# Solving a chunk's triangular system in two halves, and products that nobody reads between the stages of a delta-rule kernel

## The chip, the cores and the metric

One NeuronCore of a Trainium2 chip runs the whole program. The metric is device time in microseconds (us); the figure of a version is the median of its runs. All arithmetic is float32.

## The reference, cut to what matters

Two transformer-like layers run over one sequence of 2048 tokens of width 128. Layer 0 mixes tokens with a spiking gated delta rule of 8 heads, 64 wide; layer 1 has windowed attention; each has a feed-forward part.

```
def step(carry, ins):                       # scanned over 2048 tokens
    mem = DECAY * mem + dt;  spike = (mem > THR);  mem = mem - spike * THR
    alpha = sigmoid(at + asp * spike)
    beta  = sigmoid(bt + sum(spike * bsp))
    active = sum(abs(spike)) > 0            # the "count of spikes" per head
    alpha = where(active, alpha, 1);  beta = beta * active
    s = s * alpha
    pred = k . s
    s = s + (beta * k) (x) (v - pred)
    out = q . s
```

The kernel computes the scan of `s` in 16 chunks of 128 tokens. Within a chunk the corrections of all tokens solve a unit lower triangular system per head, T u = v - k.S, where S is the state at the chunk's start; then out = q.S + A u, and S is decayed and updated with the chunk's keys and u.

## The kernel before, in words

The program has a setup phase, a spike phase (the membrane recurrence on VectorE), the delta phase (16 chunks) and a post phase, in which groups of 512 tokens pass the output projection and feed-forward of layer 0 ("mix") beside the windowed attention and feed-forward of layer 1 of the group before ("win"). Each engine has its own list of work, written out by hand; engines meet at counting semaphores whose steps have names (`tensor_back`, `vector_front` and so on). In the delta phase each name is one step of a chunk.

One chunk on TensorE: `base` (scores within blocks of 8 tokens, L869), `blocks` (scores between blocks at the levels 8, 16, 32, 64, L892, each with half a for the even and b for the odd heads; between 16 and 32 stands the spread product, L884, which copies the near terms to all rows), `front_beta` (L851) and `front_count` (L856, the count of spikes) for the next chunk, `transposed` (L903), then `join` at 8, 16 and 32 (L920, then L929 and L931 per half) and `last_join` at 64 (L939, L945), which double the size of the inverted blocks until the whole inverse of T stands in `tt`. `state1` (L953: what the state gives for the keys; L956: end keys to rows), `solve` (L964), `seen_by_q` (L972), `state2` (L979: output; L983: update of the state) end the chunk.

VectorE does between them: `base` (L1132 masked copies, L1123 near sums, L1138 spread input), `upper` per level and half (L1160 and L1161 at 8 and 16; L1157 at 32; L1154 at 64), the substitution within blocks of 8 in seven steps `row` and `row_sum` (L1170, L1175), with an `upper` after each of the first six, `tt` (L1193), `front_z`, `front_sums` (L1057 and, as step b1, L1046), `front_late` (L1116, L1117), the joins' differences (L1203) and sums (L1209), and, in between, the next chunk's gates and keys (`front_decay` L1063 and L1066 up to `front_upper` L1107 and L1109), then `rest` (L1216), `keep` (L1222) and `update` (L1227). ScalarE copies PSUM to SBUF (L761 spread, L751 to L757 far blocks, L766 transposes, L779 joins, L788, L792, L796, output L803) and does the exponentials (L718 to L743).

In the post phase `contract` (L1741) is a product of four accumulated parts; it waits once for all of its inputs. In the last group there is only "win" work: `scores` (L1880), `weights_to_columns` (L1890), `values` (L1914), `own` (L1899), then means and variances (L1815, L1822), `last_hidden` (L1925) and `last_out` (L1741).

## Time and profile before

| | us |
|---|---|
| median of 3 runs | 1461.54 (1457.33 to 1476.28) |
| profiled execution, its own time | 1458.59 |
| profiled execution, its span | 1456.9 |

| engine | busy us | share of the span |
|---|---|---|
| TensorE products | 1115.5 | 77% |
| VectorE | 1032.8 | 71% |
| ScalarE | 625.4 | 43% |
| GpSimd | 57.4 | 4% |

The delta phase lies between about 298 and 1049 us of the span, the post phase behind it. No engine is full, and work is handed between engines many times in a chunk: the share of an engine is read per stage. A float32 product stands in the trace as two records.

### The profile page before, as it was taken

The page shows a single profiled execution, that of the slowest core. Times are in us where ns is not written, and L with a number is a line of the kernel's source. Part 1 is how long each engine was busy: PE and PEld are TensorE (multiplying, and loading weights), DVE is VectorE, ACT ScalarE, POOL GpSimd, SP SyncE. Part 2 cuts the span into 40 slices and gives each one's busy share as a digit, 9 for nine tenths or more (in the row PEclk, how much of TensorE's full clock was granted, in tenths as well). Part 3 has the DMA queues.
Part 4 walks back from the last instruction along what each step waited for, and adds up shares of the span by engine and source line. Part 5 has one row for each costly group of instructions (what it writes and reads, how often), then busy time and mean ns, then how long its engine had stood idle before and what let it go on. Part 6 is the DMA issues. An engine that isn't in the chain of part 4 may idle for free. (4 is left out here: it accounts for less than half of the span.)

```text
span 1456.9 us, 23383 instructions
## 1 busy us (share of the span) xinstructions
PE 1115.5 (77%) x7956; PEld 821.2 (56%) x7956; DVE 1032.8 (71%) x3377; ACT 625.4 (43%) x860; POOL 57.4 (4%) x74
## 2 busy tenths in 40 slices
PE   2087777228888988889888898887876888889885
PEld 1043232117777877778777787777732635446381
DVE  4779999978788787887878878788241736454451
ACT  2247677323333433334333343333333656474522
POOL 2000000010000000000000000000100102011100
PEclk9579887558999999999999999999878998998956
DMA  2002233310100100101010010110110000000000
GB/s 84 0 1 87 105 127 145 116 51 16 36 25 33 36 14 36 35 22 36 14 36 36 22 36 14 36 36 7 30 39 0 1 0 8 0 8 1 8 1 7
DMA packets 27211, 49.09 MB, mean 34 GB/s; under 512 B 4246, under 2 KB 8919, under 8 KB 27162
## 3 DMA queue, kind: packets, MB, share of 16 engines
q1 hardware_dynamic: 25642, 47.02, 9.3%
q10 hardware_dynamic: 1520, 1.48, 0.4%
q8 instruction: 23, 0.38, 0.1%
q14 instruction: 26, 0.21, 0.0%
HBM read 26.47 MB, written 22.02 MB: 33 GB/s over the span
## 5 line engine op out<-in xcount | busy, mean ns | idle before, releaser
L920 PE MATMUL ps<-delta_tm,drive 128*128 128x128 f32 x768 | 106.7, 295 | 3.9 <-DVE delta_zb L1046 3.8
L920 PEld LDWEIGHTS ps<-delta_tm,drive 128*128 128x128 f32 x768 | 98.2, 205 | 9.4 <-DVE delta_zb L1046 5.9
L931 PE MATMUL ps<-delta_tt,delta_xf 128*128 128x64 f32 x768 | 101.4, 275 | 0.0
L929 PE MATMUL ps<-delta_xf,delta_tt 128*128 128x64 f32 x768 | 99.8, 273 | 0.0
L929 PEld LDWEIGHTS ps<-delta_xf,delta_tt 128*128 128x128 f32 x768 | 94.7, 194 | 0.0
L779 ACT ACTIVATE delta_xf<-ps 128x256 f32<-128x256 f32 (+1 forms) x128 | 49.1, 383 | 106.0 <-PE ps L920 86.0
L1203 DVE TENSOR_TENSOR delta_tm<-delta_tm,ps 128x256 f32<-128x256 f32 x96 | 40.3, 419 | 76.6 <-PE ps L931 75.6
L931 PEld LDWEIGHTS ps<-delta_tt,delta_xf 128*128 128x128 f32 x768 | 93.5, 192 | 0.0
L892 PEld LDWEIGHTS ps<-delta_kq_up,delta_arena 64*128 64x128 f32 x1024 | 74.1, 225 | 22.3 <-DVE delta_diag L1161 15.1
L892 PE MATMUL ps<-delta_kq_up,delta_arena 64*128 64x128 f32 x1024 | 80.3, 317 | 1.4
L551 DVE SCALAR_TENSOR_TENSOR kept<-mem 128x32 f32<-128x32 f32 x384 | 73.2, 191 | 1.6 <-PEq L79 1.0
L556 DVE SCALAR_TENSOR_TENSOR mem<-kept,drive 128x32 f32<-128x32 f32 x384 | 73.2, 191 | 0.0
L558 DVE SCALAR_TENSOR_TENSOR mem<-kept,drive 128x32 f32<-128x32 f32 x384 | 72.9, 190 | 0.0
L554 DVE SCALAR_TENSOR_TENSOR kept<-mem 128x32 f32<-128x32 f32 x384 | 72.8, 190 | 0.0
L404 PE MATMUL ps<-prep_squares,bd 128*128 128x512 f32 x64 | 45.5, 876 | 29.8 <-ACT prep_squares L448 29.8
L766 ACT ACTIVATE delta_tm<-ps 128x512 f32<-128x512 f32 x32 | 18.2, 596 | 87.0 <-PE ps L903 87.0
L851 PE MATMUL ps<-delta_spk,beta_s 128*128 128x128 f32 x128 | 21.4, 316 | 43.1 <-DVE delta_spk L1041 43.1
L884 PE MATMUL ps<-drive,delta_block_ones 128*128 128x512 f32 x32 | 21.8, 768 | 42.0 <-DVE drive L1138 42.0
L761 ACT ACTIVATE drive<-ps 128x512 f32<-128x512 f32 x16 | 9.6, 598 | 101.8 <-PE ps L884 101.8
L1132 DVE COPY_PREDICATED delta_diag<-mask,ps 128x512 f32<-128x512 uint8 x64 | 45.0, 729 | 8.5 <-issue 8.2
L404 PEld LDWEIGHTS ps<-prep_squares,bd 128*128 128x128 f32 x64 | 17.6, 289 | 58.5 <-ACT prep_squares L448 37.2
L735 ACT ACTIVATE delta_arena<-delta_arena 128x2560 f32<-128x2560 f32 x16 | 37.4, 2338 | 23.2 <-DVE delta_arena L1085 23.2
(368 smaller groups left out, 2628.9 us busy)
## 6 DMA issues: line engine op xcount, KB each, us to landing
kq_store<-prep_unit SPq DMA_DIRECT2D x8, 1024.0 KB, 4.2
zb_store<-prep_zb_cols SPq DMA_DIRECT2D x8, 1024.0 KB, 5.7
delta_zb<-zb_store SPq DMA_DIRECT2D x16, 512.0 KB, 3.4
delta_kq<-kq_store SPq DMA_DIRECT2D x16, 512.0 KB, 3.2
v_store<-prep_v_rows SPq DMA_DIRECT2D x4, 1024.0 KB, 6.6
delta_v<-v_store SPq DMA_DIRECT2D x16, 256.0 KB, 2.6
out<-post_rows SPq DMA_DIRECT2D x4, 256.0 KB, 2.3
setup_wmod<-in_L_wmod ACTq DMA_DIRECT2D x2, 384.0 KB, 3.9
```

Source lines behind the costliest of these rows:

```text
L404: ins = eng.matmul(m.ps[:, 4 * b + c, :], m.bd[:, :], m.squares[:, 512 * c:512 * c + 512], start=True, stop=True)
L551: eng.scalar_tensor_tensor(m.kept[:, a_half], u[:, old, a_half], 1.0, u[:, old, a_half], ALU.is_gt, ALU.subtract).then_inc(step_a, 1)
L554: eng.scalar_tensor_tensor(m.kept[:, b_half], u[:, old, b_half], 1.0, u[:, old, b_half], ALU.is_gt, ALU.subtract).then_inc(step_b, 1)
L556: eng.scalar_tensor_tensor(u[:, t + 1, a_half], m.kept[:, a_half], -DECAY, d[:, t, a_half], ALU.mult, ALU.add).then_inc(step_a, 1)
L558: eng.scalar_tensor_tensor(u[:, t + 1, b_half], m.kept[:, b_half], -DECAY, d[:, t, b_half], ALU.mult, ALU.add).then_inc(step_b, 1)
L779: eng.activation(dst, src, ACT.Copy).then_inc(scalar_back, act.one(f"X{s}{x}"))
L892: ins = eng.matmul(m.ps[:, at + h % 2, P * (h // 2):P * (h // 2) + P], up_lift[s][ks, cs], m.kq_up[s][ks, :, half], start=True, stop=True)
L920: ins = eng.matmul(m.ps[:, 4 + n, P * (h % 4):P * (h % 4) + P], bt[s][:, h, :], m.tm[:, h, :], start=True, stop=True)
L929: eng.matmul(m.ps[:, 6 + n, HD * (h % 4):HD * (h % 4) + HD], m.tt[:, h, :], cols(m.xf[:, h, :], 0), start=True, stop=True)
L931: ins = eng.matmul(m.ps[:, 6 + n, 256 + HD * (h % 4):256 + HD * (h % 4) + HD], m.xf[:, h, :], cols(m.tt[:, h, :], 1), start=True, stop=True)
L1132: eng.copy_predicated(m.diag[:, hs, :, :], bc(m.mask[:, 0:P].unsqueeze(1).unsqueeze(1), [P, 2, 2, P]), ps).then_inc(vector_back, vec.one(f ...
L1203: eng.tensor_tensor(v, v, m.ps[:, 6 + n, 0:256].rearrange("p (b s) -> p b s", s=s), ALU.subtract).then_inc(vector_back, vec.one(f"TX{x}{s}"))
```

## The change

Delta phase. The join at 64 is dropped. The inverse is built only for the two halves of a chunk (64 tokens each), and the system is solved in turn: u0 = T0 rest0; w = B64 u0; rest1 -= w; u1 = T1 rest1. The join at 32 no longer makes the transposed result (its L929 products and L1203 differences go), and the products of keys and state (`seen`) move into it. The output products are split by halves. The `upper` copies of the levels 32 and 64 move from VectorE to ScalarE (`far_queries`), so that only two `upper` steps stay between the rows; `tt` is made in two halves; spikes are made a chunk ahead; some front steps move. Before the spread product two, and before the count of spikes one, 128x512 product is made that nothing reads (`unread`).

Post phase. `contract` waits for each of its four inputs in its own place; on ScalarE the copy `weights_out(i, 0)` moves ahead of part of the gate's chain; on TensorE the four `y_sums` and `values(i, 0)` change places; the last group gets `unread` products in the places of the missing mix work.

```
-JOINS = [8, 16, 32, 64]
+JOINS = [8, 16, 32]
# scalar
+            def far_queries(i):
+                eng.wait_ge(vector_back, vec.at("up16b", i))
+                for n, x in enumerate(HALVES):
+                    eng.activation(m.a_qk[0:HD, hs, HD:P], ps[0:HD, :, 1, :], ACT.Copy).then_inc(scalar_back, act.one(f"qk64{x}"))
+                for n, x in enumerate(HALVES):
+                    eng.activation(m.a_qk[0:32, hs, 32:64], ps[0:32, :, 1, 0:32], ACT.Copy)
+                    eng.activation(m.a_qk[64:96, hs, 96:128], ps[64:96, :, 1, 32:64], ACT.Copy).then_inc(scalar_back, act.one(f"qk32{x}"))
+            def solved_half(i, which):
+                ks = slice(HD * which, HD * which + HD)
+                for n, x in enumerate(HALVES):
+                    eng.wait_ge(tensor_back, pe.at(f"u{which}{x}", i))
+                    eng.activation(m.u_rows[ks, 256 * n:256 * n + 256], m.ps[ks, 4 * which + n, 0:256], ACT.Copy).then_inc(scalar_back, act.one(f"u{which}{x}"))
                 transposed(i)
+                front_gates(i + 1)
                 join(i, 8)
-                front_gates(i + 1)
...
-                last_join(i)
+                solved_half(i, 0)
                 end_rows(i)
-                solved_rows(i)
                 front_lift3(i + 1)
+                solved_half(i, 1)
# tensor
+            def unread(bank, count):
+                for _ in range(count):
+                    eng.matmul(m.ps[:, bank, :], m.block_ones[:, :], m.hh[:, 0:512], start=True, stop=True)
             def front_count(n):
-                eng.wait_ge(vector_back, vec.before("up64b", n))
+                eng.wait_ge(vector_back, vec.before("up8b", n))
+                unread(4, 1)
+                eng.wait_ge(scalar_back, act.before("qk64b", n))
                 eng.matmul(m.ps[:, 2, :], m.bd[:, :], ...)
...
                     if s == 32:
+                        eng.wait_ge(vector_back, vec.at("base0", i))
+                        unread(1, 2)
                         eng.wait_ge(vector_back, vec.at("spread", i))
                         eng.matmul(m.ps[:, 2, :], m.block_ones[:, :], spread_in, ...)
...
+                    if s < 32:
+                        for h in range(4 * n, 4 * n + 4):
+                            eng.matmul(... m.tt[:, h, :], cols(m.xf[:, h, :], 0) ...)
...
+            def solve_half(i, which):
+                ks = slice(HD * which, HD * which + HD)
+                eng.wait_ge(vector_back, vec.at("rest", i))
+                for n, x in enumerate(HALVES):
+                    eng.wait_ge(vector_back, vec.at(f"sub{x}" if which else f"XT{x}32", i))
+                    for h in range(4 * n, 4 * n + 4):
+                        ins = eng.matmul(m.ps[ks, 4 * which + n, ...], m.tt[:, h, ks], m.rest[:, HD * h:HD * h + HD], start=True, stop=True)
+            def carried(i):
+                eng.wait_ge(tensor_back, pe.at("read", i))
+                for n, x in enumerate(HALVES):
+                    eng.wait_ge(scalar_back, act.at(f"u0{x}", i))
+                    for h in range(4 * n, 4 * n + 4):
+                        ins = eng.matmul(m.ps[:, n, ...], bt[64][0:HD, h, :], m.u_rows[0:HD, HD * h:HD * h + HD], start=True, stop=True)
+            def out_half(i, which):
+                us, ts = slice(0, HD + HD * which), slice(HD * which, HD * which + HD)
+                for h in range(H):
+                    ins = eng.matmul(m.ps[ks, 6 + h % 2, c:c + HD], m.u_rows[us, HD * h:HD * h + HD], m.a_qk[us, h, ts], ...)
+            def state(i):
+                end_keys(i); solve_half(i, 0); seen_by_q(i); carried(i); out_half(i, 0)
+                eng.wait_ge(scalar_back, act.at("kend", i))
+                solve_half(i, 1)
+                eng.wait_ge(scalar_back, act.at("u1b", i))
+                out_half(i, 1); update(i)
# vector
+                for r in range(1, BASE):
+                    row(i, r)
+                    row_sum(i, r)
+                    if r < 3:
+                        upper(i, 16, HALVES[r - 1])
...
                 front_late(i)
+                front_decay(i + 1)
                 join(i, 8, "a")
+                front_mid(i + 1)
                 join(i, 8, "b")
-                front_decay(i + 1)
...
                 front_toend(i + 1)
+                rest(i)
                 join(i, 32, "a")
                 front_beta(i + 1)
                 join(i, 32, "b")
                 front_base(i + 1)
-                front_upper(i + 1, UPPER[:1])
-                rest(i)
-                front_upper(i + 1, UPPER[1:3])
+                carried(i)
+                front_upper(i + 1, UPPER[:2])
                 keep(i)
-                front_upper(i + 1, UPPER[3:])
+                front_upper(i + 1, UPPER[2:])
                 update(i)
# post phase, tensor
+            def unread(n):
+                for _ in range(n):
+                    eng.matmul(m.ps[:, 7, :], m.ones[:, :], cols(m.hT, 0), start=True, stop=True)
-            def contract(bank, w, src, done, value):
+            def contract(bank, w, src, done, value, made):
                 for c in range(4):
+                    eng.wait_ge(*made(c))
                     ins_ = eng.matmul(m.ps[:, bank, :], w[:, c, :], src[:, c, :], start=(c == 0), stop=(c == 3))
...
+                if not mix:
+                    unread(3)
```

## Rows read from the trace of the kernel before

**Rows 1.** The page: engines' busy time; the granted clock in 40 slices.
```profile
PE 1115.5 (77%) x7956; PEld 821.2 (56%) x7956; DVE 1032.8 (71%) x3377; ACT 625.4 (43%) x860; POOL 57.4 (4%) x74
PEclk9579887558999999999999999999878998998956
```
**Rows 2.** The state's tile: its update, count, durations (ns), first and last start.
```profile
L1227 DVE TENSOR_TENSOR delta_state<-delta_state,ps x16: 420/422/422, 372.3 to 1047.2; 128x256 f32<-128x256 f32 x16
```
**Rows 3.** Timeline, end of one chunk: start, duration, engine, line, operation.
```profile
778.47 0.42 DVE L1227 TENSOR_TENSOR delta_state<-delta_state,ps 128x256 f32<-128x256 f32 x1
```
**Rows 4.** Timeline, first half of the chunk that follows 822.
```profile
822.38 2.00 PE L869 MATMUL ps<-delta_kq_base,delta_km 64*128 64x256 f32 x16
822.59 0.42 DVE L1227 TENSOR_TENSOR delta_state<-delta_state,ps 128x256 f32<-128x256 f32 x1
823.56 0.73 DVE L1132 COPY_PREDICATED delta_diag<-mask,ps 128x512 f32<-128x512 uint8 x1 [0.55 <-issue]
...
829.08 1.13 PE L884 MATMUL ps<-drive,delta_block_ones 128*128 128x512 f32 x2 [2.54 <-DVE drive L1138]
...
830.87 0.17 DVE L1170 TENSOR_TENSOR drive<-drive 128x8 f32<-128x8 f32 x1
...
833.85 0.18 DVE L1170 TENSOR_TENSOR drive<-drive 128x32 f32<-128x32 f32 x1
...
834.71 0.20 DVE L1170 TENSOR_TENSOR drive<-drive 128x40 f32<-128x40 f32 x1
...
836.39 0.20 DVE L1170 TENSOR_TENSOR drive<-drive 128x56 f32<-128x56 f32 x1
836.52 0.30 PEld L856 LDWEIGHTS ps<-delta_spk,bd 128*128 128x128 f32 x2 [3.44 <-DVE delta_diag L1154]
...
836.88 1.23 DVE L1193 TENSOR_TENSOR delta_tt<-drive,delta_block_of 128x1024 f32<-128x1024 f32 x1
```
**Rows 5.** Timeline, same chunk, from the join at 32 to the next base.
```profile
849.30 1.22 DVE L1066 TENSOR_TENSOR_SCAN delta_G<-scan_keep,delta_zb 128x512 f32<-128x512 f32 x1
...
853.01 2.13 PE L920 MATMUL ps<-delta_tm,drive 128*128 128x128 f32 x16
...
854.98 1.00 PE L929 MATMUL ps<-delta_xf,delta_tt 128*128 128x64 f32 x8
...
855.82 1.06 PE L931 MATMUL ps<-delta_tt,delta_xf 128*128 128x64 f32 x8
...
862.36 1.11 PE L953 MATMUL ps<-delta_state,delta_kq_all 64*128 64x64 f32 x16
...
864.49 1.99 PE L964 MATMUL ps<-drive,delta_tt 128*128 128x64 f32 x16 [0.44 <-DVE drive L1216]
...
866.41 1.09 PE L972 MATMUL ps<-delta_kq_all,delta_state 64*64 64x128 f32 x16
866.52 0.60 ACT L796 ACTIVATE delta_u_rows<-ps 128x512 f32<-128x512 f32 x1 [1.83 <-PE ps L964]
...
868.36 0.64 PE L983 MATMUL ps<-delta_u_rows,drive 128*64 128x64 f32 x16
...
868.92 0.92 PE L869 MATMUL ps<-delta_kq_base,delta_km 64*128 64x256 f32 x6
869.13 0.42 DVE L1227 TENSOR_TENSOR delta_state<-delta_state,ps 128x256 f32<-128x256 f32 x1
```
**Rows 6.** Timeline, the spread product of another chunk.
```profile
513.71 2.07 PE L884 MATMUL ps<-drive,delta_block_ones 128*128 128x512 f32 x2 [2.54 <-DVE drive L1138]
```
**Rows 7.** Windows: stretch, length, busy per engine (instructions), clock, DMA share, GB/s.
```profile
255.00:1020.00 765.00, 607.24 (x5516) 538.55 (x5516) 626.87 (x1758) 283.57 (x492) 6.93 (x1) 0.91 0.10 33
837.60:844.40 6.80, 6.12 (x29) 5.67 (x28) 4.57 (x10) 1.87 (x5) 0.00 (x0) 0.50 0.22 77
1385.00:1421.00 36.00, 32.41 (x256) 30.94 (x256) 19.43 (x31) 7.00 (x8) 0.00 (x0) 0.50 0.00 1
1421.00:1447.00 26.00, 16.35 (x20) 4.87 (x19) 4.81 (x7) 7.98 (x12) 0.00 (x0) 0.54 0.00 0
```
**Rows 8.** Timeline, post phase: a mixed group, then the last group.
```profile
1309.28 1.98 PE L1914 MATMUL ps<-post_v,post_pt 64*128 64x32 f32 x32
...
1343.61 3.70 PE L1741 MATMUL ps<-drive,post_wff 128*128 128x512 f32 x8 [1.41 <-DVE drive L2128]
...
1390.32 3.63 PE L1914 MATMUL ps<-post_v,post_pt 64*128 64x32 f32 x32
```

More of the change, by code:

```diff
@@ L830, in _ @@
             far_blocks(NT - 1)
+            far_queries(NT - 1)
             transposed(NT - 1)
-            for s in JOINS[:-1]:
-                join(NT - 1, s)
-            last_join(NT - 1)
+            for s in JOINS:
+                join(NT - 1, s, False)
+            solved_half(NT - 1, 0)
             end_rows(NT - 1)
-            solved_rows(NT - 1)
+            solved_half(NT - 1, 1)
             output(NT - 1)
@@ L961, in solve @@
                 eng.wait_ge(vector_back, vec.at("rest", i))
-                eng.wait_ge(scalar_back, act.at("XT64b", i))
-                for h in range(H):
-                    ins = eng.matmul(m.ps[:, 5, HD * h:HD * h + HD], m.tt[:, h, :], m.rest[:, HD * h:HD * h + HD], start=True, stop=True)
-                ins.then_inc(tensor_back, pe.one("solved"))
+                for n, x in enumerate(HALVES):
+                    eng.wait_ge(vector_back, vec.at(f"sub{x}" if which else f"XT{x}32", i))
+                    for h in range(4 * n, 4 * n + 4):
+                        ins = eng.matmul(m.ps[ks, 4 * which + n, HD * (h % 4):HD * (h % 4) + HD], m.tt[:, h, ks], m.rest[:, HD * h:HD * h + HD], start=True, stop=True)
+                    ins.then_inc(tensor_back, pe.one(f"u{which}{x}"))
@@ L1014, in _ @@
             transposed(NT - 1)
-            for s in JOINS[:-1]:
+            for s in JOINS:
                 join(NT - 1, s, False)
-            last_join(NT - 1)
-            state1(NT - 1)
-            solve(NT - 1)
-            seen_by_q(NT - 1)
-            eng.wait_ge(scalar_back, act.at("solved", NT - 1))
-            state2(NT - 1)
+            state(NT - 1)
         @block.vector
@@ L1243, in _, with chunk @@
             eng.wait_ge(small_ready, 4)
-            with eng.Fori(0, NT - 1) as i:
+            def chunk(i, ahead):
                 base(i)
@@ L1275, in _ @@
             rest(NT - 1)
+            for x in HALVES:
+                join(NT - 1, 32, x)
+            carried(NT - 1)
             keep(NT - 1)
@@ L1749, in gate_in, with y_sums @@
                 eng.matmul(m.ps[0:R, 7, :], m.wu1[:, :], cols(m.hT, i), start=True, stop=True).then_inc(mix_tensor, mpe.one("g1"))
-            def y_sums(i, pair):
-                for c in range(2 * pair, 2 * pair + 2):
+            def y_sums(i, cs):
+                for c in cs:
                     if c % 2 == 0:
-                        eng.wait_ge(mix_scalar, mact.at(f"y_sq{pair}", i))
+                        eng.wait_ge(mix_scalar, mact.at(f"y_sq{c // 2}", i))
                     if c == 1:
@@ L1941, in _ @@
                     gate_in(j)
+                if not mix:
+                    eng.wait_ge(mix_scalar, mact.at("v2b", i))
+                    unread(1)
                 if win:
@@ L1944, in _ @@
                 if mix:
-                    y_sums(j, 0)
+                    y_sums(j, [0])
+                else:
+                    unread(2)
                 if win:
                     weights_to_columns(i, 0)
+                if mix:
+                    y_sums(j, [1])
+                else:
+                    unread(1)
+                if win:
                     scores(i, 2)
+                    values(i, 0)
                 if mix:
-                    y_sums(j, 1)
+                    y_sums(j, [2, 3])
                 if i == -1:
@@ L1958, in _ @@
                     gate(j)
+                if not mix:
+                    unread(1)
                 if win:
@@ L1984, in _ @@
                     gated_out(j)
+                if not mix:
+                    unread(1)
                 if win:
@@ L1988, in _ @@
                     mix_mean("n1", j)
+                else:
+                    unread(1)
                 if win:
@@ L1992, in _ @@
                     mix_var("n1", j)
+                else:
+                    unread(2)
                 if win:
                     win_var("n3", i)
+                if not mix:
+                    unread(3)
                 if mix:
@@ L2000, in _ @@
                     gelu_hidden(j, range(3, NF))
+                else:
+                    unread(2)
                 if win:
@@ L2004, in _ @@
                     gelu_out(j)
+                else:
+                    unread(2)
                 if win:
```

206 lines of the change are left out of this document (94 added, 112 removed).

## The prediction, made before the changed kernel was run

> **What bounds the kernel now.** I read the page first: TensorE is busy 77% of the span, VectorE 71%, and the granted clock is near full in the delta phase but falls to half at the end [rows 1]. Neither engine is full, so the order of hand-overs sets the time. The updates of the state (one per chunk) run from 372.3 to 1047.2, which is 15 intervals of 44.99 us [rows 2]; 16 chunks are half of the span. I then walked one chunk in the timeline. It has two parts. In the first, VectorE is the path: masked copies, the spread product and its copy, seven substitution steps, then tt; TensorE idles 2.5 us before the spread product and 3.4 us before the count [rows 4]. In the second, TensorE is the path: from the join at 32 (853.01) to the next base (868.92) it is nearly always at work, 15.91 us [rows 5]. The third thing to see is the clock. After the idle time before the count it drops to half for 6.8 us [rows 4, 7]; in another chunk it had dropped after the idle time before the spread product, which then takes 2.07 us and not 1.13 [rows 4, 6]. The chunk with that long drop takes 46.54 us (822.59 to 869.13), the one before it 44.12 [rows 3 to 5]. Last, the final group of the post phase spends 36 us at clock 0.50 with TensorE busy 32.4 of them [rows 7].
>
> **The change part by part, per chunk.**
>
> Rows. From the first substitution step to tt it is 6.01 us (830.87 to 836.88). A step with an upper copy behind it takes 0.86 us (833.85 to 834.71), one without 0.49 at most (836.39 to 836.88); I take 0.46 [rows 4]. Four upper copies leave VectorE: 4 x 0.40 = 1.6 us gained. They become six short ScalarE copies, on an engine that is busy 284 of 765 us [rows 7], and by my walk they end a good microsecond before tt does; without that cover the transposes would wait for them. Splitting tt gains nothing: the first join product waits also for b1, which stands behind tt and front_z on VectorE.
>
> The end. TensorE's list from the join at 32 becomes: X products 2.0 (853.01 to 854.98), the state's products for the keys 1.0 (L953), two XT groups 1.8 (L931 is 0.9 each), end keys 0.5: 5.3 us. Then the first solve half a. A full solve is 1.9 us for 8 heads; half of its columns as stationary operand has a near row in L983 (0.6 for 8 heads, alternating between the two column halves) and a far one in L964 (1.9). All heads of a solve half write the same half, so I take the middle, 1.0 us for 8 heads, 0.5 for 4 [rows 5]. Solve half b waits for the second XT sum, which on VectorE stands behind two front products of 0.7 us: 0.7 of waiting, then 0.5. Query products 1.0 (L972). Then w: 8 products with 64 rows and 128 columns stationary. L953 has the same shape at 1.0 us for 8 heads, but its heads alternate between the two halves of the rows; w uses the lower half alone. L931, without alternation, takes 1.8 for 8. I take 1.8 and 0.25 of hand-over, and keep 1.0 and 1.8 as ends [rows 5]. The output half is 0.6 (as L983), the second solve half 1.0, its copy by ScalarE 0.75 with hand-overs (L796 is 0.60 for twice the columns), output and update 0.6 each. The subtraction of w on VectorE is hidden behind the output half. Sum: 5.3 + 0.5 + 0.7 + 0.5 + 1.0 + 0.25 + 1.8 + 0.6 + 1.0 + 0.75 + 1.2 = 13.6 us against 15.91: 2.3 gained; with the low end of w and of the solves (0.6) 3.9 gained, with the solves at the far end 0.5 [rows 5].
>
> Costs in between. The VectorE update now stands behind four front products and comes about 1.1 us after the next base starts, not 0.2; the next masked copy starts 1.2 us after the base now (822.38 to 823.56) and would at 1.5: 0.3 lost [rows 4]. The scan (1.22) and the gate's product now run ahead of the first join's differences, and an exponential of 1 us stands on ScalarE ahead of the first join copy: I charge 0.5, between nothing and 1.2 [rows 5].
>
> Unread products. One 128x512 product is about 0.9 us at full clock (1.13 with its start, L884) and 2.07 at half [rows 4, 6]. Two fit into the 2.5 us of idle time before the spread product, one into the 3.4 us before the count: no cost at full clock. What they can give is the difference between 44.99 and a chunk with little half clock, 44.12: 0.9 us [rows 2 to 4]. Nothing at all is the other end.
>
> Sum: -1.6 - 2.3 + 0.3 + 0.5 - 0.9 = -4.0 us per chunk, -64 for 16. One more spike instruction before the loop adds 0.6. VectorE has room: its share of the phase, 627 of 765 us, is 36.9 us per chunk, and the change takes the 1.6 off (w's two subtractions replace two of the join's), so it needs 35.3 of 41 [rows 7].
>
> Post phase. The contraction after the gated hidden layer starts at 1343.61, after 1.41 us of idle time for its fourth input, and takes 3.70 [rows 8]; three of four parts can start earlier: 1.4 gained in each of 4 groups, 5.6. The same in the first group's last feed-forward, 1. The moved ScalarE copy, about 1 in each of 3 groups, 3 (none if the changed order of y_sums takes it back). In the last group the values product takes 3.63 us against 1.98 at full clock [rows 8]. The unread products stand ahead of the fourth scores and again behind own(3), not between; so I take 5 of the 36 us (ends 2 and 13), and 4.5 for the 26 us behind, at clock 0.54, with the contraction's parts included (ends 1 and 8) [rows 7]. Together -19.
>
> Total: the span 1456.9 - 64 + 0.6 - 19 = 1374.5; the profiled execution's own time lies 1.7 above its span and the median 3 above that: 1379. I give 1378.
>
> Two rules against this sum. w comes at 1.8 us since its products stay on the same rows, as L931's do [rows 5]. The Trainium skill ("TensorE: Matmul & The Clock Gate", Part 3, The mechanism) says that a weight load overlaps products in flight only where the row groups differ. By that rule w would pay load and product one after the other, roughly half as much again, 0.9 us per chunk or 14 us in all; L931's weight loads do overlap here (0.9 us for 4 heads), so I don't take it. The tail also changes between products on 64 and on 128 rows and columns more often; between L964 and L972 such a change shows no gap (864.49 + 1.99 against 866.41), so at most 0.1 us [rows 5]. The Trainium skill ("TensorEngine Tiling (Array Packing)", Key Properties) says that a change of tiling mode drains the engine; five more changes at that 0.1 would be 8 us in all, inside my range.
>
> **The rivals.**
>
> A. The clock falls in the new end of the chunk. It held there before, where the solve (L964) used all rows and columns; now nearly every product behind the join uses half of the rows or of the columns, with three hand-overs between. Speaking for it: in the last group narrow products (64 rows, 32 columns moving) fill TensorE and the clock stays at 0.50 all the same [rows 7, 8]. Against it: L953 to L983 are narrow too and keep their full-clock durations [rows 5]. The price is the 0.9 not gained and a long drop, 46.54 - 44.12 = 2.4: 3.3 x 16 = 53, so 1431.
>
> B. The solve in turn is dearer. Three round trips (u0, w, u1) between TensorE, ScalarE and VectorE replace one, and VectorE's subtraction can get stuck behind front products. With solves at the far end and half a microsecond more of waiting, 1.5 x 16 = 24: 1402.
>
> C. The other side: unread products at half clock. TensorE takes its list in order, so they delay the spread product when they don't fit. If the clock is at half from the chunk's end on, base (twice 2.0), two block levels (about as much again) and two unread products (twice 2.07) end 12.1 us after the base starts; the spread product starts now after 6.7 (822.38 to 829.08) [rows 4, 6]. That is 5.4 late, per chunk -4.0 + 0.9 + 2.4 + 5.4 = +4.7, and with the post phase as forecast 1461 + 75 - 19 = 1517. It decides as soon as the clock is low over the whole front of most chunks; the unread products themselves work against that.
>
> D. The last group keeps its full clock throughout: 12 more gained, 1366, or less with w at its low end, down to 1350.
>
> **How the numbers follow.** Forecast 0.54 (1362 to 1395, which takes in unread products that gain nothing, 14 us); A 0.23; B 0.13; C 0.06; D at its low end 0.04. A difference of under 2% (29 us), about what a measurement here tells from no change, ends at 1432. A lies across it, half and half. Faster by over 2%: 0.54 + 0.13 + 0.04 + 0.115 = 0.82; within 2%: 0.12; slower: 0.06. The range takes in the forecast, B and most of A: 1355 to 1436.
>
> **What would show it.** Interval between updates: 41 us. First substitution step to tt: 4.4. Join at 32 to next base: 13.6; w near 1.8 for 8 heads (1.0: my row was the wrong one). Idle time before spread and count under 1 us with the clock at full. Rival A shows as clock 0.5 with L869 near 4 us, C as a spread product that starts over 8 us after the base, B as idle time at the w and u1 products. If VectorE is busy for all of a chunk, the list on it is the bound and all my TensorE terms are moot.

## The result, and the profile after

The changed kernel takes 1399.83 us (median of 4 runs, 1398.28 to 1401.53); the kernel before took 1461.99 in the same comparison. The ratio is 0.956, with a 95% interval of 0.949 to 0.963. That is faster by over 2% and inside my range of 1355 to 1436, but 22 us above the forecast of 1378 and outside the 1362 to 1395 that I gave the forecast by itself. The profiled run took 1398.87 us, with a span of 1397.1.

The page of the changed kernel, engines' busy time and the granted clock in 40 slices, and the update of the state:

```profile
PE 1104.1 (79%) x8084; PEld 774.3 (55%) x8084; DVE 1013.1 (73%) x3297; ACT 635.0 (45%) x940; POOL 56.9 (4%) x74
PEclk9589878657999999999999999999878898997988
L1249 DVE TENSOR_TENSOR delta_state<-delta_state,ps x16: 420/422/422, 368.8 to 1001.0; 128x256 f32<-128x256 f32 x16
```

The clock digits of the end went from 56 to 88 [rows 1]. The interval between updates is (1001.0 - 368.8) / 15 = 42.15 us against 44.99 [rows 2], where I forecast 41. The first update comes 3.5 us sooner, the delta phase ends 46.2 us sooner (63 forecast), and what is behind it takes 13.6 us less (19 forecast).

The timeline of the changed kernel, one chunk's end and the next one's start (start, duration, engine, line):

```profile
819.51 2.20 PE L936 MATMUL ps<-delta_tm,drive 128*128 128x128 f32 x16
...
821.64 1.11 PE L958 MATMUL ps<-delta_state,delta_kq_all 64*128 64x64 f32 x16
...
822.68 2.00 PE L950 MATMUL ps<-delta_tt,delta_xf 128*128 128x64 f32 x16
...
824.52 0.61 PE L965 MATMUL ps<-ident,delta_k_end 128*128 128x128 f32 x4
...
825.05 0.68 PE L975 MATMUL ps<-drive,delta_tt 128*64 128x64 f32 x8
...
826.17 0.68 PE L975 MATMUL ps<-drive,delta_tt 128*64 128x64 f32 x8 [0.44 <-DVE delta_tt L1224]
...
826.78 1.09 PE L992 MATMUL ps<-delta_kq_all,delta_state 64*64 64x128 f32 x16
...
828.01 1.86 PEld L984 LDWEIGHTS ps<-delta_u_rows,drive 64*128 64x128 f32 x16 [0.38 <-ACT drive L802]
828.01 1.99 PE L984 MATMUL ps<-delta_u_rows,drive 64*128 64x64 f32 x16
829.15 0.42 DVE L1239 TENSOR_TENSOR drive<-drive,ps 64x256 f32<-64x256 f32 x1 [1.30 <-PE ps L984]
829.93 0.68 PE L1001 MATMUL ps<-delta_diag,delta_u_rows 64*64 64x64 f32 x16
...
830.55 1.15 PE L975 MATMUL ps<-drive,delta_tt 128*64 128x64 f32 x16
...
832.16 0.69 PE L1001 MATMUL ps<-delta_diag,delta_u_rows 128*64 128x64 f32 x16 [0.47 <-ACT delta_u_rows L798]
...
832.67 0.64 PE L1010 MATMUL ps<-delta_u_rows,drive 128*64 128x64 f32 x16
...
833.05 0.68 DVE L1137 TENSOR_TENSOR delta_kq_up<-delta_kq,delta_arena 128x512 f32<-128x512 f32 x1
833.24 1.13 PE L885 MATMUL ps<-delta_kq_base,delta_km 64*128 64x256 f32 x8
833.65 0.42 DVE L1135 TENSOR_TENSOR delta_arena<-delta_beta_k,delta_arena 128x256 f32<-128x256 f32 x1
833.99 0.68 DVE L1137 TENSOR_TENSOR delta_kq_up<-delta_kq,delta_arena 128x512 f32<-128x512 f32 x1
834.70 0.42 DVE L1249 TENSOR_TENSOR delta_state<-delta_state,ps 128x256 f32<-128x256 f32 x1
835.05 0.73 DVE L1160 COPY_PREDICATED delta_diag<-mask,ps 128x512 f32<-128x512 uint8 x1
...
835.18 1.14 PE L885 MATMUL ps<-delta_kq_base,delta_km 64*128 64x256 f32 x8 [0.80 <-DVE delta_state L1249]
...
840.58 0.70 PE L901 MATMUL ps<-drive,delta_block_ones 128*128 128x512 f32 x1 [0.57 <-DVE drive L1166]
```

Read it against [rows 5] and then [rows 4]. The end is as forecast: 13.73 us from the join at 32 to the base (819.51 to 833.24), against 15.91 before. The step to see is the last: VectorE still has front products to do when TensorE is through. The update (L1249) starts 1.46 us after the base, where it was 0.2 before; the second half of the base waits 0.80 us for it, the first masked copy comes 1.8 us after the base (1.2 before), and the spread product 7.3 us after it (6.7 before).

The granted clock is the other thing. In the changed kernel it falls to half for 3.4 us at a time, mostly about 15 us after the update (the join at 8 then takes 3.68 us and not 2.0, see the row below) or about 38 us after it, in the narrow products of the end. Six of the 15 intervals show no such stretch. The windows of the changed kernel (borders; width, busy time of each engine, clock, DMA share, GB/s): two stretches at half clock, twelve intervals of the delta phase, then the three spans between writes of a group's rows in the post phase; and two rows of its timeline:

```profile
850.00:853.40 3.40, 3.40 (x17) 3.40 (x18) 2.25 (x5) 2.38 (x3) 0.00 (x0) 0.50 0.24 54
873.90:877.30 3.40, 2.93 (x44) 2.63 (x41) 3.40 (x8) 1.51 (x3) 0.00 (x0) 0.50 0.00 0
413.00:919.60 506.60, 454.08 (x4392) 382.43 (x4392) 425.99 (x1044) 215.71 (x433) 0.00 (x0) 0.97 0.09 31
1162.60:1245.60 83.00, 74.00 (x466) 43.40 (x464) 42.79 (x61) 48.75 (x64) 10.07 (x9) 0.92 0.01 4
1245.60:1333.30 87.70, 78.97 (x464) 45.67 (x462) 43.04 (x61) 48.65 (x62) 9.97 (x9) 0.86 0.01 4
1333.30:1394.40 61.10, 53.85 (x366) 34.52 (x362) 30.10 (x43) 17.43 (x22) 0.80 (x1) 0.86 0.02 5
...
849.87 3.68 PE L936 MATMUL ps<-delta_tm,drive 128*128 128x128 f32 x16 [0.99 <-DVE delta_zb L1074]
...
1297.29 3.60 PE L1785 MATMUL ps<-drive,post_wff 128*128 128x512 f32 x8
```

Before, the same three spans took 82.8, 84.5 and 74.3 us. Windows of the kernel before:

```profile
1212.50:1295.30 82.80, 73.37 (x464) 41.17 (x463) 43.27 (x61) 48.81 (x63) 9.98 (x9) 0.94 0.01 4
1295.30:1379.80 84.50, 75.07 (x468) 42.69 (x464) 43.57 (x61) 48.86 (x63) 10.08 (x9) 0.92 0.01 4
1379.80:1454.10 74.30, 54.62 (x334) 38.92 (x329) 30.37 (x43) 17.04 (x21) 0.73 (x1) 0.59 0.02 4
```

So the last group gained 13.2 us and the stretch ahead of the first rows 3.7 (it holds two contractions of the four), and the two groups between lost 3.4, though the gated contraction starts without idle time now (1297.29; it had 1.41 [rows 8]).

### The profile page after: what moved, and what is told of

The parts are those of the page before. It is cut to its first block and busy times, and to the rows that moved or that the text cites. A ratio compares the mean times of both kernels' runs of the same rounds, so it can differ in the third digit from the quotient of the medians.

```text
span 1397.1 us, 23429 instructions
## 1 busy us (share of the span) xinstructions
PE 1104.1 (79%) x8084; PEld 774.3 (55%) x8084; DVE 1013.1 (73%) x3297; ACT 635.0 (45%) x940; POOL 56.9 (4%) x74
## 5 line engine op out<-in xcount | busy, mean ns | idle before, releaser
L790 ACT ACTIVATE delta_xf<-ps 128x256 f32<-128x256 f32 x96 | 36.5, 380 | 130.2 <-PE ps L936 130.0
L909 PEld LDWEIGHTS ps<-delta_kq_up,delta_arena 64*128 64x128 f32 x1024 | 63.0, 193 | 13.8 <-DVE delta_diag L1179 12.1
L948 PE MATMUL ps<-delta_xf,delta_tt 128*128 128x64 f32 x512 | 68.3, 277 | 0.6
L909 PE MATMUL ps<-delta_kq_up,delta_arena 64*128 64x128 f32 x1024 | 66.3, 281 | 0.0
L948 PEld LDWEIGHTS ps<-delta_xf,delta_tt 128*128 128x128 f32 x512 | 64.2, 197 | 2.4 <-issue 2.4
L798 ACT ACTIVATE delta_u_rows<-ps 64x256 f32<-64x256 f32 x64 | 24.2, 378 | 86.1 <-PE ps L975 85.1
L860 PE MATMUL ps<-delta_spk,beta_s 128*128 128x128 f32 x128 | 19.7, 300 | 43.3 <-DVE delta_spk L1069 43.3
L1218 DVE TENSOR_TENSOR delta_tm<-delta_tm,ps 128x256 f32<-128x256 f32 x64 | 26.5, 415 | 36.6 <-PE ps L950 36.6
L885 PE MATMUL ps<-delta_kq_base,delta_km 64*128 64x256 f32 x256 | 38.0, 430 | 18.2 <-DVE delta_kq_base L1129 11.0
L1224 DVE SCALAR_TENSOR_TENSOR delta_tt<-ps,first_neg,delta_tt 128x256 f32<-128x256 f32 x96 | 46.0, 479 | 4.7 <-PE ps L950 4.7
L866 PE MATMUL ps<-hh,delta_block_ones 128*128 128x512 f32 x96 | 48.7, 617 | 0.0
```

The costliest lines, as they stand in the source:

```text
L866: eng.matmul(m.ps[:, bank, :], m.block_ones[:, :], m.hh[:, 0:512], start=True, stop=True)
L909: ins = eng.matmul(m.ps[:, at + h % 2, P * (h // 2):P * (h // 2) + P], up_lift[s][ks, cs], m.kq_up[s][ks, :, half], start=True, stop=True)
L948: eng.matmul(m.ps[:, 6 + n, HD * (h % 4):HD * (h % 4) + HD], m.tt[:, h, :], cols(m.xf[:, h, :], 0), start=True, stop=True)
L1224: eng.scalar_tensor_tensor(v, m.ps[:, 6 + n, 256:512].rearrange("p (b s) -> p b s", s=s), m.first_neg[:, LEVELS.index(s):LEVELS.index(s) + ...
```

## The experiments

All times are medians; "interval" is the mean over the 15 intervals between updates in the profiled run, and the spans are that run's too. The kernel before took 1462 to 1463 in each comparison. A profiled run is not always a typical one: that of 1 took 1397.64 us and that of 10 1394.75, both below their medians, and that of 7 took 1460.14, above its median.

| kernel | us | interval | post spans (second to last group) |
|---|---|---|---|
| before | 1462 | 44.99 | 82.8, 84.5, 74.3 |
| changed | 1399.8 | 42.15 | 83.0, 87.7, 61.1 |
| 1 no unread products in the delta phase | 1403.2 | 42.08 | 83.0, 87.8, 61.1 |
| 2 none in the post phase | 1410.1 | 42.20 | 83.0, 84.4, 73.7 |
| 3 old order in the post phase | 1407.4 | 42.36 | 88.7, 88.7, 62.6 |
| 4 more unread products | 1396.9 | 42.03 | 83.0, 87.8, 61.1 |
| 5 update sooner | 1380.2 | 40.94 | 83.0, 87.8, 61.1 |
| 6 second join sum sooner too | 1377.8 | 40.90 | 83.0, 87.7, 61.1 |
| 7 before, with the delta unread products | 1453.6 | 44.35 | 88.8, 88.8, 74.7 |
| 8 unread products in every group | 1394.4 | 42.18 | 80.0, 81.6, 62.6 |
| 9 all together | 1370.1 | 40.87 | 81.5, 79.9, 63.5 |
| 10 as 5, no unread in the delta phase | 1401.1 | 41.90 | 83.0, 84.4, 61.1 |
| 11 as 9, one more product in the end | 1370.9 | 40.78 | 81.6, 81.3, 62.4 |
| 12 as 11, that product twice as wide | 1371.2 | 40.92 | 81.5, 79.9, 63.5 |

**1. Without the unread products of the delta phase.**

```
 def front_count(n):
-    unread(4, 1)
 ...
-    eng.wait_ge(vector_back, vec.at("base0", i))
-    unread(1, 2)
```

> The changed kernel without the unread wide products of the delta phase (two ahead of the spread product, one ahead of the count of spikes); the rest is as changed, the three products are left out and nothing reads them. Theory: they hold the clock at full in the front of the chunk. Without them the half-clock stretches of the kernel before come back there (6 to 8 us or 15 us after the update of the state), as in the forecast 0.9 us per chunk: interval between updates 43.0 us instead of 42.15, time about 1414 us. Rival: they fill idle time and nothing else; the clock falls elsewhere as often, the interval stays at 42.15 within 0.2 and the time at 1400 within 3. Second rival: they cost time, since they stand ahead of the spread product; without them the spread product starts less than 6.7 us after the base and the time is under 1397.

1403.24 us (1397.64 to 1406.39), 3.4 more than the changed kernel, whose own runs lie inside that spread, and the interval is the same within 0.1. The theory's 1414 and 43.0 fell. Half clock is back 6 to 8 us after the update in 11 of 15 intervals; further stretches begin once at 17 us, five times at 38 to 41, and at 12 in the last interval. In all it fills 65 us between the first and the last update, and 44 in the changed kernel. So the products do take half clock away, but what is left costs as much: 0.6 us an interval above the 41.55 of an undisturbed one, and 0.5 here. Windows of this kernel, an interval with 3.4 us of half clock 7.5 us after the update and one with none:

```profile
411.20:452.70 41.50, 35.88 (x360) 31.40 (x360) 35.34 (x87) 17.77 (x37) 0.00 (x0) 0.96 0.09 32
537.40:578.90 41.50, 34.46 (x360) 29.92 (x360) 35.36 (x87) 17.88 (x37) 0.00 (x0) 1.00 0.09 32
```

From update to update they take 41.54 and 41.56 us (411.16 to 452.70 and 537.38 to 578.94): half clock costs nothing in that place, where VectorE is the path. A stretch that begins at 6.3 us catches the spread product and does cost time.

**2. Without those of the last group.** `unread` of the post phase issues nothing.

> The changed kernel without the unread wide products of the last group of the post phase (they are left out; the waits of the contractions and the new orders stay). Theory: those products take the last group from 61 us of half clock to 17. Without them the clock stays at half from the values products to the end, the last group takes 71 us (74.3 before, less 1.4 to 3 for contraction parts that start earlier) instead of 61.1, and the time is about 1410 us. Rival: the earlier values product and the parted contractions carry the gain; the last group stays under 64 us and the time under 1403.

1410.06 us, as the theory said. The last group takes 73.7 us and not 61.1, almost what it took before. Windows of this kernel, the last two groups:

```profile
1245.80:1330.20 84.40, 75.67 (x465) 43.95 (x464) 43.07 (x61) 48.67 (x62) 10.01 (x9) 0.90 0.01 4
1330.20:1403.90 73.70, 54.75 (x334) 39.17 (x330) 30.35 (x43) 17.09 (x21) 0.75 (x1) 0.58 0.01 4
```

Clock 0.58 where the changed kernel has 0.86. The parted contractions and the new order alone give 0.6 us there. The group ahead of it is 3.3 shorter than in the changed kernel, with no difference in its instructions: its clock is 0.90 and not 0.86.

**3. The old order in the groups that mix.**

```
-    y_sums(j, [0])
+    y_sums(j, [0, 1])
     ...
     weights_to_columns(i, 0)
-    y_sums(j, [1])
     ...
     scores(i, 2)
-    values(i, 0)
     y_sums(j, [2, 3])
     ...
+    values(i, 0)
```

(The conditions around these calls are left out. ScalarE's gate chain stands again ahead of its first weights copy.)

> The changed kernel with the order of the kernel before in the groups that mix (sums of squares two by two, the first values product behind them, ScalarE's gate chain ahead of the first weights copy); contractions in parts and the unread products stay. Theory: the new order is why the three middle groups gained nothing: in the group from 1245 to 1333 us the fourth scores came 22.75 us after the rows, 19.46 before the change. With the old order each of those groups is 1.4 to 3 us shorter and the time is 1391 to 1396 us. Rival: the order is neutral and what ate the gain is half clock (24 us of it in that group against 14); then the groups stay at 83 and 87 us and the time at 1400 within 2.

1407.37 us, 7.5 more: both theories fell. With the old order the groups take 88.7 us each. But that is less a price of the order than it looks, as 7 shows.

**4. More unread products in idle places of the chunk.**

```
     front_count(i + 1)
+    unread(4, 1)
     transposed(i)
+    unread(4, 1, 256)
     join(i, 8)
 ...  # in the end, 128x256 each: ahead of the second group of the first
 ...  # solve half, of carried(i), and of the second out_half
```

> The changed kernel with more unread products in idle places of the chunk: one of 128x512 ahead of the transposes, and one of 128x256 each ahead of the first join, ahead of the second group of the first solve half, ahead of the products that carry the first half over, and ahead of the second output half. Their price at full clock is at most 0.1 us each, 0.5 per chunk. Theory: in the five intervals of the changed kernel that show no half clock a chunk takes 40.95 us, in the others 42.8: the whole shortfall against the forecast of 41 is the clock, that falls after the idle time before the first join and in the narrow products of the end. With these places filled the interval is 41.0 to 41.4 us, time 1382 to 1388. Rival: half clock comes back elsewhere or the added products delay more than they hold: interval 42.2 or more, time 1400 or more.

1396.86 us: my theory that the whole shortfall was clock fell here. Windows of this kernel, twelve intervals:

```profile
412.80:918.00 505.20, 479.35 (x4512) 388.92 (x4512) 424.69 (x1045) 214.93 (x433) 0.00 (x0) 1.00 0.09 31
```

The clock is 1.00 throughout, and each interval is still 42.10 us (505.20 / 12). The added products cost 0.6 of it: 34.28 us from spread product to update product, 33.66 in chunks of the changed kernel with full clock. That leaves 41.5 as the full-clock interval of the changed kernel, the same as in run 1's interval with no half clock. In the trace the spread product stood 7.26 us after the base in every chunk. The chunks of the changed kernel that I had taken as models, 40.95 us from base to base, had 6.7 only because half clock had held TensorE back until VectorE was through.

**5. One front pair ahead of w's subtractions.**

```
     front_base(i + 1)
+    front_upper(i + 1, UPPER[:1])
     carried(i)
-    front_upper(i + 1, UPPER[:2])
+    front_upper(i + 1, UPPER[1:2])
```

> The changed kernel with one pair of VectorE's front products (level 8) moved ahead of w's two subtractions, where VectorE idles 1.30 us; it stands behind them now. Theory: the run with more unread products never had half clock in the chunks and still took 42.10 us, so full clock is not the whole story. There the spread product starts 7.26 us after the base, in the changed kernel 6.7 only where half clock had delayed the base: the update of the state, 1.46 us behind the base on VectorE behind the front products, holds up the masked copies. With the pair moved the update comes under 0.5 us after the base and the spread product 6.7 us after it; the interval falls by 0.5, time 1391 to 1395. Rival: the pair delays the subtractions and the second solve half by as much as it gives; interval 42.1 and time 1400 as it was.

1380.18 us, 19.7 less than the changed kernel, and more than I expected. Timeline of this kernel around a base, and its windows over twelve intervals:

```profile
779.16 0.68 DVE L1137 TENSOR_TENSOR delta_kq_up<-delta_kq,delta_arena 128x512 f32<-128x512 f32 x1
...
779.35 2.13 PE L885 MATMUL ps<-delta_kq_base,delta_km 64*128 64x256 f32 x16
779.88 0.42 DVE L1249 TENSOR_TENSOR delta_state<-delta_state,ps 128x256 f32<-128x256 f32 x1
...
780.53 0.73 DVE L1160 COPY_PREDICATED delta_diag<-mask,ps 128x512 f32<-128x512 uint8 x1 [0.23 <-issue]
...
786.06 1.13 PE L901 MATMUL ps<-drive,delta_block_ones 128*128 128x512 f32 x2 [0.63 <-DVE drive L1166]
...
411.70:902.60 490.90, 444.88 (x4394) 369.79 (x4392) 425.36 (x1044) 215.16 (x433) 0.00 (x0) 1.00 0.10 32
```

The update is 0.53 us behind the base, the base's idle time is gone, the spread product comes 6.71 us after the base, and the interval is 40.91 in each of the twelve. Of the 1.2 us per chunk 0.64 are the update's delay: the spread product came 7.34 us after the base where the update was late (840.58 less 833.24), and comes 6.71 after it now. The cleanest pair for it is 1 and 10, which differ by this move alone: their intervals without half clock take 41.55 us (1) and 40.92 (10). The other 0.6 are half clock, which is gone from these twelve intervals altogether.

**6. The second join sum sooner,** on top of 5. VectorE's product of beta and the keys moves behind `join(i, 32, "b")`.

> As the kernel with the update sooner, and the product of beta and the keys (0.69 us on VectorE) moved behind the second sum of the join at 32, for which the second group of the first solve half waits 0.44 us. Theory: TensorE's end of the chunk is a chain, and 0.44 us of the 13.7 from the join to the base go: interval 0.4 lower than with the update sooner alone, time 1385 to 1389. Rival: what is pushed back on VectorE (the product, the base's and the upper ones) arrives as late as TensorE's gain, the update again stands over 1 us behind the base, and the time is that of the update sooner alone within 2 us.

1377.78 us (1373.74 to 1379.84), better than expected against the changed kernel, but against 5 it gives 2.4 us and not 6, and the two spreads overlap (5 ran from 1376.14 to 1383.25). At full clock an interval is 40.26, 0.65 less than in 5. But in 9 of 15 intervals half clock is back 15 us after the update, and those take 41.1 to 41.5. The mean is 40.90: the clock took back what the list gave.

**7. The kernel before, with the three unread products of the delta phase only.**

> The kernel before with only the three unread wide products of the delta phase (two ahead of the spread product, one ahead of the count). Theory: they take away the half-clock stretches 6 to 8 and 15 us after the update, and nothing else: the interval falls from 44.99 to 44.1 as I reckoned in the forecast, time 1448 us. Rival, which the run without them speaks for: half clock in a stretch where TensorE waits for VectorE costs nothing, and the products give nothing; interval 44.9 to 45.1 and time 1462 within 4.

1453.58 us, ratio 0.993 (0.989 to 0.998), between the theory and its rival. The interval falls by 0.64 to 44.35, so here the products do give something. Eight intervals show no half clock and take 44.12 to 44.18 us; those with 3.4 us of it 13.7 us after the update take 44.6. In the kernel before, the intervals with 3.4 us of it about 8 us after the update, behind the spread product, took 44.11 to 44.16: there it costs nothing. The post phase holds the kernel before's instructions, unchanged; windows of the three spans:

```profile
1203.50:1292.30 88.80, 79.72 (x468) 46.40 (x464) 42.60 (x61) 48.97 (x64) 10.03 (x9) 0.87 0.01 4
1292.30:1381.00 88.70, 79.62 (x464) 46.30 (x462) 42.60 (x61) 48.87 (x62) 9.93 (x9) 0.87 0.01 4
1381.00:1455.70 74.70, 54.97 (x334) 39.09 (x330) 30.35 (x43) 17.10 (x22) 0.78 (x1) 0.59 0.01 4
```

The same lists took 82.8 and 84.5 us in the profile of before, at clock 0.94 and 0.92. So 4 to 6 us in a middle group hang on where half clock comes to lie, with nothing changed in it. That is the size of what I had wanted to read there, in 3 too, where both groups ran at clock 0.85.

**8. Unread products in every group of the post phase.**

```
+    eng.wait_ge(mix_vector, mvec.at("g0", j)); unread(1)
     weights_to_columns(i, 0)
 ...
+    eng.wait_ge(mix_scalar, mact.at("y_ln3", j)); unread(1)
     scores(i, 3)
```

> The changed kernel with two more unread products in each of the three groups of the post phase that mix and attend: one ahead of the first weights' transposes (idle 2.12 us), one ahead of the fourth scores (idle 1.94 us). Theory: in those groups the parted contractions do save their 1.4 us of idle time, but half clock of 14 to 24 us per group eats it; the groups took 83.0, 87.7 and 61.1 us. With the clock held the first two come to 77 to 80 us each and the time to 1386 to 1390. Rival: the idle times are ScalarE's and VectorE's and the half clock lies beside them; then the groups stay at 83 and 84 to 88 us and the time at 1400 within 3.

1394.42 us, 5.4 less. In the profiled run (7.9 less) 3.2 are gained ahead of the first rows and 9.1 in the two middle groups; 1.5 are lost in the last group, 2.4 ahead of the first update and 0.5 behind it, where the edit touches nothing. Windows of this kernel:

```profile
1162.30:1242.30 80.00, 72.91 (x468) 40.88 (x468) 42.85 (x61) 48.70 (x64) 10.24 (x9) 0.96 0.02 4
1242.30:1324.00 81.70, 74.61 (x472) 42.66 (x468) 42.95 (x61) 48.73 (x63) 10.34 (x9) 0.94 0.01 4
1324.00:1386.50 62.50, 56.76 (x366) 37.24 (x359) 30.08 (x43) 17.30 (x21) 0.72 (x1) 0.81 0.02 5
```

Clock 0.96 and 0.94 instead of 0.92 and 0.86: half clock had hidden a gain in the middle groups. How much of one can be read from groups with an equal amount of half clock: with 13.7 us of it a group took 84.4 before and 83.0 in the changed kernel, with 23.9 us 88.8 (7) and 87.7, with 10.2 us 82.8 before and 81.6 here. So the changes to these groups are worth 1.0 to 1.5 us each against the kernel before, and the 9.1 that came on top here are clock: 17.0 us of half clock in the two groups instead of 37.6.

**9. All together:** 5, 6 and 8, and the first two products of 4.

> The changed kernel with the update sooner, the second join sum sooner, one unread product of 128x512 ahead of the transposes and one of 128x256 ahead of the first join, and the two more unread products in each middle group of the post phase. Theory: with the sum sooner a chunk takes 40.26 us at full clock and 41.45 where the clock falls 15 us behind the update; the two unread products hold it there at no cost (in the kernel with more of them the times from count to transposes to join stayed the same), so every interval is 40.3 us: 0.6 x 15 = 9 us less than 1377.8, and the middle groups give 5 to 8 more. Time 1360 to 1366. Rival: the clock falls somewhere else in the shorter chunk, as it did in the changed kernel, and gives 0.6 back: 1370 to 1374.

1370.07 us (1367.79 to 1371.01), ratio 0.935 (0.930 to 0.939): the best version, 30 us under the changed kernel. The rival for the delta phase holds: half clock moved on, to 37 to 38 us after the update in 7 of 15 intervals, and the mean is 40.87 against 40.28 in the undisturbed ones.

**10. The update sooner, without the unread products of the delta phase.** The edits of 5 and 1.

> The kernel with the update sooner, without the three unread products of the delta phase (left out). It asks whether those products are worth anything once VectorE is no longer late. Theory A: in the changed kernel they moved half clock from 6 to 8 us after the update, where it cost 0.3 us, to 15 and 38 us, where it cost over 1; with the update sooner nothing falls behind, so here too half clock would come back at 6 to 8 us, and cost 0.3 or less: interval 41.0 to 41.3, time 1380 to 1385. Theory B: they are what keeps the clock at full in that kernel; without them the clock falls at 15 and 38 us as well and the interval is 41.8 or more, time 1392 or more.

1401.07 us, but from 1385.21 to 1412.12; without the highest of the six the median is 1400.03 and the highest 1402.29. Windows of this kernel, from shortly before the end of the first interval to that of the fifth, then eight more, and one of these by itself:

```profile
411.70:588.90 177.20, 152.69 (x1483) 133.78 (x1483) 144.79 (x355) 73.63 (x147) 0.00 (x0) 0.90 0.09 30
588.90:916.30 327.40, 278.07 (x2884) 240.42 (x2882) 283.73 (x697) 143.25 (x289) 0.00 (x0) 0.99 0.09 32
629.80:670.70 40.90, 34.57 (x362) 29.87 (x360) 35.44 (x87) 17.91 (x37) 0.00 (x0) 1.00 0.09 32
```

The second to fifth intervals take 42.99 to 44.31 us, the eight behind them 40.91 to 40.94, with the same instructions. So theory B holds in the main: with the update sooner the unread products are worth about 20 us, and the time is steadier with them (5 ran from 1376.14 to 1383.25; here five of six runs lie between 1385.21 and 1402.29). The profiled run here was one of the faster ones, so its interval of 41.90 shows only part of the 20.

**11 and 12. One more product ahead of the second output half**, 128x256 in 11, 128x512 in 12, on top of 9.

> The kernel with everything together, and one more unread product of 128x256 ahead of the second output half, where TensorE idles 0.47 us for ScalarE's copy. Theory: in the kernel with everything together the clock fell in 6 of 15 intervals 37.2 to 37.7 us behind the update, in the narrow products of the chunk's end, and the mean was 40.87 us where the others take 40.28. A full-width product there holds it at a price of 0.1 us: every interval 40.3 to 40.4, time 1360 to 1364. Rival: the product is too little, or comes too late in the end, and the clock falls all the same: interval 40.8 to 41.0, time 1369 to 1372.

> As the kernel with everything together and one more product in the end, but with that product 128x512: at full clock it takes about 0.9 us where 0.47 are idle, so it delays the second output half by some 0.45. Theory: what holds the clock is what TensorE does; the clock stays at full in all intervals, each at 40.7 us, and the time is 1366 to 1370, the price of a product that doesn't fit. Rival: the narrower one did not hold the clock and this one does; then it beats that kernel, else it loses to it by 0.35 us a chunk, 6 us in all.

1370.85 and 1371.18 us: no difference to 9 that these runs can tell. In 11 the product costs 0.08 and does not hold the clock (half clock in 5 intervals, 41.6 us each). In 12 it does, but for one interval (42.4): the others up to the last two are 40.8 us each, where an undisturbed one of 9 takes 40.3, so it costs the 0.5 that it saves.

## Why the prediction was near, and where it failed

**The rows** held: from the first substitution step to tt it is 4.49 us (4.4 forecast). **The end** held: 13.73 us against 13.6, with w at 1.9 (828.01 to 829.93; 1.8 forecast). The sum in the front part, +0.5 for scan and exponential, was 0.45 (11.21 us from the first join to the join at 32, 10.76 before).

**The rule on weight loads.** In w the starts of loads and products take turns, 56 ns apart (load at 828.338, product at 828.394, load at 828.449), and w takes 1.99 us. The same shape with its heads on alternating halves of the rows (L958) starts two of each in the time of one here and takes 1.11. The records overlap in both cases, since a product's lasts 272 ns here, so that the loads' 1.86 us lie beside the products' 1.99 decides nothing. The Trainium skill ("TensorE: Matmul & The Clock Gate", Part 3, The mechanism) has loads overlap with products in flight only across row groups, and the starts in this trace agree with it. My 1.8 came from L931, which stays on the same rows too and whose loads and products also take turns at 56 ns. It held that price already. To leave out a second 0.9 was right; my reason, that L931's loads overlap, was not.

**Changes between 64 and 128 rows or columns** are not free, though I read that from [rows 5], and 828.01 + 1.99 against 829.93 reads the same way: the record of the last product runs on beyond the next start. By the starts, w's last product stands at 829.734 and the load behind it at 829.934, 0.20 us, where a load inside w follows a product by 0.06. The other changes of this end, apart from those that fall in a wait, show 0.15 to 0.20; so each costs 0.09 to 0.15 us, a little more than my 0.1 at most. The Trainium skill ("TensorEngine Tiling (Array Packing)", Key Properties) says that a change of tiling mode drains the engine, and the trace agrees. The end has eight such changes where it had five; the 13.73 us hold them.

**The step that failed first is "0.3 lost" for the place of the update.** I had the wait right, but its size too small: the update 1.1 us behind the base forecast, 1.46 measured, and with it the masked copy at 1.8 and not 1.5. The price is 0.64 per chunk (41.55 against 40.92 in the undisturbed intervals of 1 and 10), 10 us in all and not 5. Experiment 5 shows that this is the cause: with one pair moved the delay goes, and the spread product is back at 6.7.

**The second is "-0.9" for the clock.** I read it from the kernel before, as 44.99 against 44.12, and 44.12 is indeed what an interval of that kernel takes at full clock (7). What failed is that all of it would come back: in the changed kernel half clock lay elsewhere and cost 0.6 per chunk (42.15 less 41.55), and the three products changed next to nothing of its cost (1). So the term is 0.87 less 0.6, -0.27. The sum by the measured terms is -1.5 - 2.2 + 0.45 + 0.64 - 0.27 = -2.9, against -2.84 measured and -4.0 forecast. Rival A was thus partly right: the clock does fall in the new end, and also ahead of the first join, for 0.6 us a chunk and not 3.3. It was not needed, though: with the update in time (5) it did not fall at all in twelve intervals, and the kernel took 1380, 2 above my forecast. Rivals B, C and D did not come about: no idle time at the w or u1 products beyond 0.5 us, and the spread product never over 7.7 us behind the base, but for the first chunk (10.1, as before the change). That the time came out 2 us from rival B's 1402 is chance, then, and it is in my range because the range was drawn wide enough for B and A. In the last group 17 us of half clock are left.

**The post phase**, -13.6 against -19. By spans the 19 were 4.8 ahead of the first rows (two contractions, the gelu, a copy), 2.4 in each middle group, and 9.5 in the last. Measured were 3.7, -3.4 for the two middle ones together, and 13.2, nearly all of that the unread products' (12.6 by experiment 2). So in the last group my term for these products was too small. What failed is the middle groups' 4.8: at an equal amount of half clock they gained 1.0 to 1.5 each and not 2.4 (see 8), and they had 37.6 us of half clock between them instead of 23.9, which took back that gain and 3.4 more. How much of the 1.0 to 1.5 is the parted contraction and how much the new order, no run separates.

What stays open: what decides which chunks fall to half clock. The place moved with each edit (6 to 8, 12 to 17, 37 to 41 us behind the update), and in 10 the same instructions ran both ways.

## What to carry to other kernels

When you shorten the engine that is the path at the end of a loop body, look at what the other engine still has to do there, and at every instruction queued ahead of the one that the next turn waits for. One pair of products moved into an idle place gave 20 us here, about half of it directly and half by the clock, and that is more than the whole shortfall of the delta phase (17). And a term for the clock read from half-clock stretches of the old kernel isn't a gain of the new one: check with a version that never falls, and ask what its full-clock time is.

## What the runs showed of the hardware

Half clock also comes with TensorE at work: it was busy for 3.40 of 3.40 us in the stretch at 850.0, in the join at 8, behind transposes and 0.99 us of idle time. Behind the spread product, where VectorE is the path, it costs nothing (intervals of 44.12 us with 3.4 us of it, in the kernel before, and of 44.12 without, in 7); 14 us behind the update the same 3.4 us cost 0.5 (44.6, in 7). The same instructions took 82.8 or 88.8 us in a post group, at clock 0.94 and 0.87, and 40.9 or 44.3 us in a chunk of one run. Unread products that fill idle time narrow that spread: 7 us between the runs of 5, 17 us without them between five of the six runs of 10, and the sixth lies 10 us above those. Products on the same rows and their weight loads took turns, 0.11 us for a load and a product (w, 1.99 us for 8 heads); on alternating halves of the rows two such pairs started in that time (L958, 1.11 us). A change between 64 and 128 rows or columns cost 0.09 to 0.15 us.
